# A mixture-of-experts and attention kernel: the memset between GpSimd's indirect DMAs, 128x256 in place of 128x512

## The chip, the cores and the metric

The kernel runs on one core of a Trainium2 chip. The metric is the device time of one execution in microseconds (us). In the profile the engines are called PE (TensorE), DVE (VectorE), ACT (ScalarE), POOL (GpSimd) and SP (SyncE); SP only issues DMAs. A name such as "SPq" is an engine's instruction queue, "PEld" is the loading of PE's weights.

## The reference

There are eight batch rows x of 1024 tokens and 256 features. Three steps are added to x in turn: half of a sparse feed-forward layer (FFN), an attention layer, and half of the same sparse FFN again, each on a layer-normalized input.

```python
x = x + 0.5 * ffn(layernorm(x))
x = x + attn(layernorm(x))          # windows of 64, plus 256 routed tokens a row
x = x + 0.5 * ffn(layernorm(x))

def ffn(x):                          # 8 experts of width 128, the best 2 of each token
    w = softmax(x @ router_w + router_b)
    mask = top_2_of(w) / sum(top_2_of(w))
    h = gelu(einsum('btd,nde->btne', x, W1) + b1)
    return sum_over_experts((einsum('btne,nef->btnf', h, W2) + b2) * mask)
```

## The kernel before, in words

The first FFN is computed sparsely, and this is where the change lies. The eight rows are dealt with in three batches, `BATCH = ((0, 2), (2, 5), (5, 8))`. For each row ACT and DVE normalize the tokens into `xb`, PE computes the router's logits, and DVE works out for every token the two places (`spot`) at which it shall stand in a list sorted by expert (`row_spots`, last line L1513). POOL then scatters the row to HBM: `send(r, i)` writes 128 tokens of `xb` to `spots_d` with one indirect DMA (L1952), 16 of them for a row (8 tiles of tokens, 2 experts each). Behind each send stands `pause`, which zeroes the scratch tile `apart`; nothing reads that tile.

When all sends of a batch have landed (`sent`, L613), SP loads blocks of 256 tokens, all of one expert, into `xin` (L617). The batches give 23, 31 and 31 blocks, 85 in all. For each block PE transposes (L863), multiplies by W1 (L872) and by W2 (L890), ACT computes the gelu (L1197), DVE adds the bias into `yout` (L1578), and SP stores it to `made_d` (L623). The loads run three blocks ahead through four buffers. `fetch(b, i)` on POOL gathers the results of row b back with an indirect DMA (L1976); the 16 fetches of row 0 are followed by `pause` too, those of later rows are not.

All engines go through one list of "ticks". Block s has tick 24 + s; row r starts at tick `ROW_AT[r]`, with `ROW_AT = (0, 6, 12, 18, 26, 33, 41, 49)`, its positions come 9 ticks and its sends 11 ticks later. So rows 0 to 2 are prepared before the first block and rows 3 to 7 between blocks. On SP the block load of tick t + 3 stands ahead of the row load of the same tick t. POOL has no other work than the sends between 35 and 251 us, and takes them in order of the rows.

After the blocks, from about 351 us, the attention layer runs (PE is the fullest engine), with scatters (`hs_d`, L1992) and fetches without `pause`, and then the second FFN, which is computed densely.

Of the kernel before, what the change touches and what calls it, by code (L numbers as in the profile page):

```python
# [8 lines left out]
F32 = mybir.dt.float32  # L9
# [9 lines left out]
P = 128  # L19
# [19 lines left out]
def build(nc, x_in, gamma_h, wq_h, wkv_h, wo_h, ln_g, ln_b, wqkv, wo_l, rt_q, rt_kv,  # L39
          router_w, router_b, w1, b1, w2, b2, out):  # L40
    pe, act, dve, pool, sp = nc.tensor, nc.scalar, nc.vector, nc.gpsimd, nc.sync
    ROWS, N, D = x_in.shape
# [27 lines left out]
    with ctx:  # L70
# [7 lines left out]
        def room(nbytes):  # L78
            at_ = top[0]
            top[0] += -(-nbytes // 32) * 32  # L80
            assert top[0] <= nc.sbuf_usable_end, (name_of_last[0], top[0], nc.sbuf_usable_end)
            return at_
# [3 lines left out]
        def at(name, shape, dt, offset):  # L86
            return nc.alloc_sbuf_tensor_at(name, shape, dt, offset=offset)
# [87 lines left out]
        xf_off = room(2 * C * 2 * P * 4)  # L175
# [55 lines left out]
        assert top[0] <= xf_off, (top[0], xf_off)  # L231


        apart = at("apart", [P, 2 * D], F32, xf_off)
        xb = [at(f"xb{i}", [P, T, D], F32, off) for i, off in enumerate((xt_off, xt_off + T * D * 4, y_off, yr_off + T * (D + 1) * 4))]
        zeros = at("zeros", [P, BT, D], F32, xt_off + 4 * TG * D * 4)
        assert 4 * TG * D + BT * D <= 2 * C * PADDED
# [1905 lines left out]
```

How the kernel before makes its waits and increments, by code:

```python
        def sent(engine, n):  # L575
            for r in range(*BATCH[n]):
                engine.wait_ge(s_sc[r % 4], 32 * T * (r // 4 + 1))
# [1 line left out]
        def made(engine, n):  # L580
            end = FIRST[n] + BLOCKS[n]
            for i in range(4):
                engine.wait_ge(s_bst[i], 16 * ((end - 1 - i) // 4 + 1))
# [10 lines left out]
            def row_load(r):  # L595
                if r >= 4:
                    sp.wait_ge(s_sc[r % 4], 32 * T * (r // 4))
                sp.dma_start(xb[r % 4][:, :, :], x_v[r]).then_inc(s_xa[r % 4], 16)
# [1 line left out]
            def pads(n, i):  # L600
                if n == 0 and i == 0:
                    sp.wait_ge(s_const, CONST)
                sp.wait_ge(s_tab, NTAB * (n + 1))
                for e in range(E // 2 * i, E // 2 * (i + 1)):
                    row = value(sp, pad_row[n][0:1, e:e + 1], 0, SPARE[n] - BLK)
                    sp.dma_start(spots_d[n][bass.ds(row, BLK), :].rearrange("(p s) d -> p s d", s=BT), zeros[:, :, :]).then_inc(s_zero, 16)
# [1 line left out]
            def block_load(s_):  # L609
                n = batch_of(s_)
                if s_ == FIRST[n]:
                    sent(sp, n)
                    sp.wait_ge(s_zero, 16 * E * (n + 1))
                if s_ >= 4:
                    sp.wait_ge(s_bT, s_ - 3)
                row = value(sp, block_row[n][0:1, s_ - FIRST[n]:s_ - FIRST[n] + 1], 0, SPARE[n] - BLK)
                sp.dma_start(xin[s_ % 4][:, :, :], spots_d[n][bass.ds(row, BLK), :].rearrange("(p s) d -> p s d", s=BT)).then_inc(s_bld[s_ % 4], 16)
```

## Time and profile before

| what | value |
|---|---|
| time, median of 3 runs | 2064.11 us (2062.43 to 2066.58) |
| the profiled execution | 2061.01 us, span 2059.2 us |
| busy over the span | PE 1875.1, DVE 1388.5, ACT 1203.6, POOL 1172.0 us |
| memsets of `apart` | 144, 78.0 us in all |
| indirect DMAs of `send` | 128, first start 35.32 us, last start 250.21 us |
| blocks | 85, first transpose 95.33 us, last at 346.3 us |

The span runs from the first instruction to the last. Busy time is the sum of an engine's instructions, without waits. An engine's idle time is shown in brackets before an instruction, with an arrow to what released it.

### The profile page before, as it was taken

To read this page: it belongs to the slowest core of one execution; us is meant where nothing else is said; L and a number is where in the kernel's file an instruction comes from. 1 tells how busy PE (TensorE), PEld (TensorE's weight loads), DVE (VectorE), ACT (ScalarE), POOL (GpSimd) and SP (SyncE) were. 2 spreads that over 40 slices of the span, in tenths; PEclk is the share of its full clock that TensorE was granted. 3 is DMA by queue.
4 is the path that set the end of the run, shared out by engine and by line. 5 is a ranking of instruction groups with operands and counts; after the bars stand their busy time and mean duration, and the time that the engine had idled before them with its cause. 6 is when DMAs were issued, how large, how long until landed. Compare 5 with 4: busy or idle time off the path is not lost.

```text
span 2059.2 us, 38092 instructions
## 1 busy us (share of the span) xinstructions
PE 1875.1 (91%) x11764; PEld 1398.7 (68%) x11764; DVE 1388.5 (67%) x4771; ACT 1203.6 (58%) x2974; POOL 1172.0 (57%) x1356
## 2 busy tenths in 40 slices
PE   3488899889989989989989989989999999999998
PEld 1166678656656666666666666666666788888887
DVE  5355457756855865875874875775754488888887
ACT  5487567565565565565566566566555555555554
POOL 3999852662772782782682683583453444444444
PEclk8599999999999999999999999999999999999999
DMA  6688887200310310310310220220121111111110
GB/s 200 248 267 289 275 267 251 67 27 1 100 40 1 98 42 1 95 45 1 93 47 1 81 55 5 77 57 8 37 63 82 38 42 42 42 42 42 36 38 21
DMA packets 103841, 168.15 MB, mean 82 GB/s; under 512 B 13249, under 2 KB 64857, under 8 KB 102745
## 3 DMA queue, kind: packets, MB, share of 16 engines
q1 hardware_dynamic: 80600, 112.91, 16.8%
q0 software_dynamic: 20736, 52.52, 8.1%
q8 instruction: 97, 1.59, 0.3%
q14 instruction: 104, 0.84, 0.1%
q10 hardware_dynamic: 2304, 0.28, 0.1%
HBM read 80.33 MB, written 85.34 MB: 80 GB/s over the span
## 4 chain that ended last, share of the span: by engine, by line
PE 51%; DVE 16%; POOL 10%; issue 10%; ACT 9%; DMA 4%; ACTq 0%; SPq 0%; DVEq 0%; POOLq 0%
PE bank L730 7%; PE bank L732 6%; PE bank L731 6%; PE bank L1022 4%; PE bank L1011 4%; PE bank L982 4%; PE bank L993 4%; PE bank L953 3%; PE bank L890 2%; ACT prob L1319 2%; PE bank L872 2%; POOL prob L2005 2%; DVE st L1412 2%; POOL spots_d L1952 2%; PE bank L984 2%
## 5 line engine op out<-in xcount | busy, mean ns | idle before, releaser
L2005 POOL TENSOR_TENSOR prob<-prob,rden 128x512 f32<-128x512 f32 x320 | 337.6, 1056 | 453.8 <-DVE rden L1798 450.2
L1319 ACT ACTIVATE prob<-prob,nmax 128x256 f32<-128x256 f32 x512 | 256.0, 502 | 391.3 <-DVE nmax L1780 383.5
L1780 DVE CUSTOM_DVE_ANT_0 prob<-bank,mask 128x256 f32<-128x256 f32 x512 | 195.3, 417 | 103.3 <-PE bank L982 97.3
L1666 DVE SCALAR_TENSOR_TENSOR xb<-bank,gate,xb 128x256 f32<-128x256 f32 x512 | 211.8, 476 | 55.6 <-PE bank L732 55.1
L1932 POOL TENSOR_TENSOR hl<-hf,hh 128x512 fp32r<-128x512 f32 x128 | 164.7, 1291 | 113.8 <-ACT hh L1122 109.1
L982 PE MATMUL bank<-kT,qT 64*128 64x256 f32 x1024 | 211.2, 431 | 14.3 <-DVE nmax L1780 13.6
L993 PE MATMUL bank<-ident,prob 128*128 128x128 f32 x1280 | 198.8, 278 | 16.1 <-POOL prob L2005 16.1
L993 PEld LDWEIGHTS bank<-ident,prob 128*128 128x128 f32 x1280 | 154.3, 142 | 73.7 <-POOL prob L2005 26.5
L1121 ACT ACTIVATE hf<-bank,b1s 128x512 f32<-128x512 f32 x128 | 88.2, 689 | 171.2 <-PE bank L732 167.7
L1792 DVE COPY probT<-bank 128x512 f32<-128x512 f32 x160 | 110.0, 688 | 113.7 <-PE bank L993 112.8
L1011 PE MATMUL bank<-probT,V 128*64 128x128 f32 x2048 | 169.7, 287 | 9.0 <-ACT oT_s L1335 7.1
L1992 POOL DMA_INDIRECT hs_d<-yr,place x128 | 130.0, 1016 | 43.4 <-issue 31.0
L1952 POOL DMA_INDIRECT spots_d<-xb,spot x128 | 126.3, 987 | 49.4 <-DVE spot L1513 28.4
L1011 PEld LDWEIGHTS bank<-probT,V 128*64 128x64 f32 x2048 | 108.2, 137 | 64.5 <-issue 61.3
L730 PE MATMUL bank<-w,hh 128*128 128x256 f32 x512 | 146.6, 286 | 3.7 <-POOL hl L1932 2.6
L982 PEld LDWEIGHTS bank<-kT,qT 64*128 64x128 f32 x1024 | 94.0, 186 | 77.7 <-issue 47.1
L732 PE MATMUL bank<-w,hh 128*128 128x256 f32 x512 | 144.7, 283 | 0.0
L731 PE MATMUL bank<-w,hl 128*128 128x256 f32 x512 | 144.5, 282 | 0.0
L1812 DVE TENSOR_TENSOR x<-bank,x 128x256 f32<-128x256 f32 x64 | 27.0, 422 | 147.0 <-PE bank L1022 147.0
L1578 DVE TENSOR_TENSOR yout<-bank,b_all 128x512 f32<-128x512 f32 x85 | 58.1, 690 | 100.5 <-PE bank L890 62.0
L1022 PE MATMUL bank<-wol,oT_s 128*128 128x256 f32 x512 | 125.8, 388 | 0.0
L730 PE MATMUL bank<-xt_hi,wqkv_hi 128*128 128x512 f32 x256 | 114.1, 446 | 0.0
(256 smaller groups left out, 5044.7 us busy)
## 6 DMA issues: line engine op xcount, KB each, us to landing
xin<-spots_d SPq DMA_DIRECT2D x85, 256.0 KB
made_d<-yout SPq DMA_DIRECT2D x85, 256.0 KB
x<-in_L_attn_x SPq DMA_DIRECT2D x8, 1024.0 KB
x_d<-x SPq DMA_DIRECT2D x8, 1024.0 KB, 4.5
xb<-x_d SPq DMA_DIRECT2D x16, 512.0 KB, 3.9
out<-xb SPq DMA_DIRECT2D x16, 512.0 KB, 3.0
xb<-in_L_attn_x SPq DMA_DIRECT2D x7, 1024.0 KB, 6.7
spots_d<-zeros SPq DMA_DIRECT2D x24, 256.0 KB
```

Of the source, the lines that this page charges most:

```text
L730: pe.matmul(o, w[0], x[0], start=start, stop=False)
L731: pe.matmul(o, w[1], x[0], start=False, stop=False)
L732: return pe.matmul(o, w[0], x[1], start=False, stop=stop)
L982: ins = pe.matmul(bank[g % NS][:, 0:KEYS], qT[hs, hp, t * P:(t + 1) * P], kT[hs, hp, t * P:t * P + KEYS], start=True, stop=True)
L993: ins = pe.transpose(bank[3 + j % 2][:, (2 * h + kk) * P:(2 * h + kk + 1) * P], prob[j % NP][:, h, kk * P:(kk + 1) * P], ident[:, :])
L1011: ins = pe.matmul(bank[5][h * DH:(h + 1) * DH, hp * P:(hp + 1) * P], V[:, t + kk, hs] if t < T else hv[:, kk, hs], probT[j % 2][:, 2 * h + ...
L1022: ins = pe.matmul(bank[tb][:, 0:D], oT_s[:, ch, :], w[:, ch, :], start=(ch == 0), stop=(ch == HC - 1))
L1319: act.activation(prob[j % NP][:, h, :], src, ACT.Exp, bias=nmax[:, j % 4, h:h + 1], scale=-1.0 if light else 1.0, accum_out=den[:, j % 4, ...
L1666: dve.scalar_tensor_tensor(out=x, in0=bank[ob][:, (t % 2) * D:(t % 2 + 1) * D], scalar=gate[:, k % 2, t, e:e + 1], in1=x, op0=ALU.mult, op ...
L1780: ins = dve.tensor_tensor_reduce(prob[j % NP][:, h, :], bank[g % NS][:, 0:KEYS], mask[:, which, :], -1.0, 3e38, ALU.add, ALU.min, nmax[:, ...
L1952: pool.indirect_dma_start(spots_d[batch_of_row(r)], bass.IndirectOffsetOnAxis(spot[:, r, c, t:t + 1], 0), xb[r % 4][:, t, :], None).then_i ...
L2005: pool.tensor_tensor(prob[j % NP][:, :, :], prob[j % NP][:, :, :], rden[:, j % 4, :].unsqueeze(2).broadcast_to([P, 2, KEYS]), ALU.mult).th ...
```

## The change

The scratch tile `apart` is declared with 256 elements a partition and not 512. The memset in `pause` writes the whole tile, so each of its 144 executions writes half as much. Nothing else changes: no semaphore, no order, no DMA.

```diff
-        apart = at("apart", [P, 2 * D], F32, xf_off)
+        apart = at("apart", [P, D], F32, xf_off)
```

with D = 256, and its only use:

```python
            def pause(n):
                if n > 0:
                    pool.wait_ge(s_apart, n)
                pool.memset(apart[:, :], 0.0).then_inc(s_apart)
```

## Rows read from the trace of the kernel before

**Rows 1.** The page: busy tenths of POOL in 40 slices of the span.

```profile
POOL 3999852662772782782682683583453444444444
```

**Rows 2.** Windows by stage: length, busy time of each engine, clock, DMA share, GB/s.

```profile
35.00:92.00 57.00, 21.33 (x92) 10.99 (x90) 29.49 (x100) 31.30 (x57) 51.34 (x65) 0.62 0.50 186
92.00:182.00 90.00, 77.43 (x403) 52.80 (x403) 44.50 (x144) 65.41 (x129) 81.06 (x109) 0.96 0.82 273
```

**Rows 3.** Waits of SP's queue, 0 to 370 us: total, times, longest.

```profile
SPq L613 <- DMA spots_d<-xb,spot: 29.1, 2, 22.9
```

**Rows 4.** Timeline of POOL: start, duration, instruction, idle time before it.

```profile
35.32 2.20 POOL L1952 DMA_INDIRECT spots_d<-xb,spot  x1 [28.40 <-DVE spot L1513]
...
250.21 0.96 POOL L1952 DMA_INDIRECT spots_d<-xb,spot  x1 [0.17 <-issue]
...
254.55 0.20 POOL L2058 MEMSET xt_hi<- 128x128 f32 x1 [2.84 <-DMA spots_d<-xb,spot]
```

**Rows 5.** The chain that ended last, 88 to 96 us: start, duration, what.

```profile
87.88 0.97 POOL spots_d L1952
...
91.95 0.02 SPq L613
...
92.46 2.82 DMA xin<-spots_d
...
95.33 1.11 PE bank L863 x4
```

**Rows 6.** POOL's groups by form: count, busy us, mean ns, idle before.

```profile
L1958 POOL MEMSET apart<- 128x512 f32 x144 | 78.0, 541 | 0.1
...
L2027 POOL MEMSET zeros<- 128x512 f32 x1 | 0.5, 514 | 0.0
...
L2078 POOL MEMSET kT<- 128x256 f32 x1 | 0.3, 308 | 0.0
```

**Rows 7.** Timeline of POOL where no memset stands between indirect DMAs.

```profile
364.39 0.96 POOL L1992 DMA_INDIRECT hs_d<-yr,place  x1 [0.30 <-ACT yr L1237]
365.66 1.05 POOL L1992 DMA_INDIRECT hs_d<-yr,place  x1 [0.30 <-ACT yr L1237]
```

**Rows 8.** Timeline of DVE: positions of rows 1, 3, 4 and 7.

```profile
51.77 0.46 DVE L1513 CAST spot<-spot_f 128x16 uint32<-128x16 f32 x1
...
111.42 0.17 DVE L1513 CAST spot<-spot_f 128x16 uint32<-128x16 f32 x1
...
139.37 0.17 DVE L1513 CAST spot<-spot_f 128x16 uint32<-128x16 f32 x1
...
221.07 0.45 DVE L1513 CAST spot<-spot_f 128x16 uint32<-128x16 f32 x1
```

**Rows 9.** Timeline of SP's queue: a store, and the load of block 23.

```profile
165.65 0.32 SPq L623 DMA_DIRECT2D made_d<-yout  x1
172.90 0.35 SPq L617 DMA_DIRECT2D xin<-spots_d  x1
```

**Rows 10.** Timeline of PE: two block transposes that waited for their load.

```profile
182.23 0.66 PE L863 MATMUL bank<-ident,xin 128*128 128x128 f32 x4 [0.75 <-DMA xin<-spots_d]
...
273.09 0.68 PE L863 MATMUL bank<-ident,xin 128*128 128x128 f32 x4 [2.40 <-DMA xin<-spots_d]
```

**Rows 11.** The chain that ended last, 263 to 279 us.

```profile
263.31 9.73 DMA xin<-spots_d
...
273.77 1.71 PE bank L890 x4
...
277.60 0.87 PE bank L890 x4
```

**Rows 12.** Windows around the start of batch 2.

```profile
240.00:255.00 15.00, 12.46 (x61) 10.64 (x60) 3.64 (x6) 6.79 (x15) 11.00 (x19) 0.89 1.00 341
255.00:275.00 20.00, 17.60 (x95) 15.15 (x94) 5.34 (x8) 11.08 (x25) 17.85 (x26) 0.96 0.95 321
...
273.00:277.00 4.00, 3.91 (x13) 3.09 (x14) 0.78 (x2) 0.60 (x1) 3.58 (x6) 0.57 1.02 390
```

## The prediction, on record before the result

> **What bounds the kernel now.** I read the slices of the page first, because the edit touches one GpSimd instruction and the question is where that engine sets the pace. POOL is nearly full in slices 2 to 5 and half idle later [rows 1]. A table by stage follows: from 35 to 92 us POOL is busy 51.3 of 57 us while PE has 21.3; from 92 us on POOL is as full (81.1 of 90 us), but PE has 77.4 of the 90 and the blocks run, with the DMA engines busy 0.82 of the time [rows 2]. So there are two regimes, and a GpSimd saving is worth something different in each.
>
> The waits of the DMA queue on SP name the place of the first regime: SP waits at L613 (`sent`, in front of the first block load of a batch) for the scatters, twice, 29.1 us in all, 22.9 us the longer [rows 3]. The timeline of POOL shows what it waits for. The first send starts at 35.32, the 128th at 250.21 with a gap of 0.17 us before it [rows 4], and each is a DMA_INDIRECT with one `apart` memset behind it. (250.21 - 35.32) / 127 = 1.692 us per send. Batch 0 has two rows, 32 sends. The chain of waits says that this reaches the end: the last send of batch 0, its DMA, the first `xin` load (2.82 us), the first block transpose at 95.33 [rows 5], before which PE had nothing to do. From there on the ticks (the 85 blocks and the preparation of rows 3 to 7) stand in program order behind that first block, so what the start gains, all that follows gains, unless something else ends a wait.
>
> **The memset's price.** The changed tile has 256 elements a partition. `apart` at 512 takes 0.541 us on average; a halo of `kT` is a memset of 128x256 f32 at 0.308; `zeros`, 128x512, took 0.514 on a quiet chip [rows 6]. Saving: 0.541 - 0.308 = 0.233 us. Bounds: 0.514 - 0.308 = 0.206, if the 0.027 that `apart` takes above `zeros` stays; 0.541 / 2 = 0.27, if all of it scales. I take 0.233, the row with exactly the new shape. As a page has it: the Trainium skill (GPSIMD Engine Reference, Elementwise — side-by-side cycle accounting) puts a simple body at 1.03 cycles an element at 1.2 GHz; an estimate from it is 256 x 1.03 / 1.2 GHz = 0.220 us, by which the first term below would be 6.8 us; the trace's own two shapes give 0.206 to 0.233 and decide.
>
> **Does the period shrink by it?** Where no memset stands between, as at 364.39 and 365.66, indirect DMAs start 1.27 us apart, 0.96 us of work and a gap of 0.30 [rows 7]. That is the nearest floor. The new period would be 1.692 - 0.233 = 1.459 us, above 1.27, so nothing seen here stops it. All of the saving then shortens POOL's sequence.
>
> **Batch 0 (the main term).** Between the starts of the first and the last of 32 sends lie 31 memsets: 31 x 0.233 = 7.2 us (6.4 and 8.4 by the bounds). The inputs are there: POOL now comes to row 1 at 35.32 + 16 x 1.459 = 58.7, and row 1's positions stand at 52.2 [rows 8]. SP's wait of 22.9 us leaves 15.7 before anything else on its queue can come last. The first block starts at 88.1 in place of 95.3. The load of row 4 stands behind the first block load on SP, so it moves along too.
>
> **Batch 1.** Rows 3 and 4 have positions (L1513) only after PE has done blocks: 111.6 and 139.5 us, row 7's at 221.5 [rows 8]. Moved by 7.2 these are 104.4 and 132.3. POOL reaches row 3 at 35.3 + 48 x 1.459 = 105.4, so it doesn't wait; it is through row 3 at 128.7 and waits 3.6 us for row 4. Here POOL stops being the bound. The last send of batch 1 starts at 132.3 + 15 x 1.459 = 154.2 and has landed about 4 us later, as the last of batch 0 did (87.88 to 91.95), at 158.3. SP now finishes its store at 165.98 and can load block 23 only at 172.90 [rows 9]; moved by 7.2 it comes at 158.8. The 6.2 us wait of SP goes. For PE it was worth little, as loads run three blocks ahead: one wait of 0.75 us at 182.23 [rows 10]. Term: 0.75 us, between 0 and 0.75.
>
> **Batch 2.** Its sends have landed when the halo memset starts at 254.55 [rows 4], and the load of block 54 is issued at 263.31 [rows 11]: 8 us of slack already, so sends that end sooner give nothing by themselves. With the last row's positions at 221.5 - 8.0 = 213.5 its last send starts at 235.4 and the slack is 15 us. 16 fetches (L1976) come next on POOL. 14 run now from 255.6 to 278, over the load of block 54, which takes 9.73 us; PE waits 2.40 us for it [rows 10, 11] and then runs 0.57 of its clock from 273 to 277 us [rows 12], the lower of its two levels (1.2 of 2.4 GHz) for most of it: 1.71 us for a group of four against 0.87 once warm [rows 11], so two such groups cost 1.7 more. The stall is worth 2.4 + 1.7 = 4.1 us. After the change the fetches run from 240.4, 1.42 us apart, to 260.2, and the load of block 54 is issued at 255.3: they lie over 5 of its 9.7 us, not over all; the load of row 0's x for the attention, which `attn_load` issues at tick 74, 4 blocks before (1024 x 256 values of 4 bytes, 1 MB), stays beside it. Bounds 0 and 4.1; nearer to no change, as the large load stays: 1.0 us.
>
> **After 351 us** there is no `apart` left and POOL's work is the same; the stage moves as a whole. The last 16 pauses, in the fetches, lie under the blocks (PE idle there is for block 54 alone): nothing for them.
>
> **Sum:** 7.2 + 0.75 + 1.0 = 9.0 us. The profiled execution took 2061.0 us (span 2059.2 and 1.8 around it), so 2052.0 on its own scale; the median of the runs shown is 3.1 us above, at 2064.1, and so **2055.1**.
>
> **The rivals.**
> (a) The stall at block 54 goes entirely, through a load freed of fetches: 7.2 + 0.75 + 4.1 = 12.1 us, and 13.3 with the upper memset bound: 2050.8 to 2052. For it: the DMA engines are at 0.95 to 1.0 in this stretch [rows 12], so 10 fetches less beside it count. Against: the x load of 1 MB stays. 0.17.
> (b) A part is given back. Between 240 and 255 us the DMA engines are at 1.00 [rows 12]; sends 16% denser (1.692 / 1.459) leave the block loads less. One more stall like block 54's costs 4.1: 9.0 - 4.1 = 4.9 us, 2059.2. For it: PE does wait for `xin` at two places [rows 10]. Against: 4 us pauses between rows appear from row 4 on, and total bytes are equal. 0.16.
> (c) The edit doesn't do what it says: the period is held by something else, descriptor making for instance, and the gap grows as the memset shrinks. Within 1 us of 2064.1. Against it stand the 1.27 us pairs [rows 7]; for it, that a gap after an indirect DMA is 0.30 and after the memset 0.16, of which 0.14 x 31 = 4.3 us could come back; with that partial form the gain is 9.0 - 4.3 = 4.7. Whole form 0.07.
> (d) Slower: the denser sends of batches 1 and 2 make PE run out of loaded blocks repeatedly, between 97 and 235 us, each time dropping its clock as at block 54. To lose by more than 4.1 us it must give back 13.1: four stalls of 4.1, 2064.1 - 9.0 + 16.4 = 2071.5. For it: the DMA engines at 0.82 [rows 2]. Against: with sends 1.692 us apart the wait at 182.23 was 0.75 us and cost no clock. 0.04. The page that would make it so: the Trainium skill (DMA: Bandwidth & Descriptors, Queues, rings and completion order) says that each DMA engine takes turns between the queues that have work, packet by packet, so the scatters' queue takes its share from SP's. The trace agrees that they compete, 9.73 us for block 54's load against 2.82 for the first.
>
> **How the numbers follow.** My forecast, a gain of 7 to 11 us (2053 to 2057), has 0.56, and the rivals the rest. The range reaches from (a) with the upper bound, 2050.5, over (b) and the partial form of (c), to 2060.0; what it leaves out is (c) whole, (d) and the tails. 0.2% is 4.1 us, about what this kernel's measurement can tell from no change. Faster takes the forecast, (a) and most of (b), 0.86; same takes (c) and the weak end of (b), 0.10; slower (d), 0.04.
>
> **What would show it.** `apart` at about 0.31 us and POOL's period at 1.46 (else (c)). SP's first wait for the scatters about 15.7 us in place of 22.9, the first transpose near 88; the second such wait gone. POOL idle some 3 us before row 4's sends. The blocks ended 8 to 12 us earlier, and the whole stage after them as long as before. If the blocks' stage is longer than now, counted from its own first transpose, it is (b) or (d), and the place is where PE waits for `xin`. The prediction is wrong above all if that stage stretches, or if a gap takes the memset's place.

## The result, and the profile after

The changed kernel took 2076.19 us (median of 8 runs, 2070.67 to 2080.96) where the kernel before, run beside it, took 2062.5 us (2060.2 to 2066.58): a ratio of 1.0066, 95% interval 1.005 to 1.0083. It is 13.7 us slower; 2055.1 us was forecast. The profiled execution took 2080.96 us with a span of 2079.2.

The same kernel, run again in two later sets of runs, gave two answers, and this matters for all that follows: 2078.95 us against 2062.96 in one set (1.0076, 1.0056 to 1.0096) and 2055.56 against 2060.64 in the other (0.9978, 0.9964 to 0.9991). So the document first reads the profile of the run on record, which lost time, then tells how the two answers differ in their traces.

**The start went nearly as forecast.** The groups of POOL's instructions on `apart` after, with the shortest, median and longest duration in ns, and its timeline at the first and at the second send:

```profile
L1958 POOL MEMSET apart<- x144: 317/326/338, 37.2 to 312.5; 128x256 f32 x144
```

```profile
34.96 2.20 POOL L1952 DMA_INDIRECT spots_d<-xb,spot  x1 [28.03 <-DVE spot L1513]
37.21 0.32 POOL L1958 MEMSET apart<- 128x256 f32 x1
37.69 0.97 POOL L1952 DMA_INDIRECT spots_d<-xb,spot  x1 [0.16 <-issue]
```

The memset went from 0.541 us to 0.326, a saving of 0.215 (0.233 forecast), and the gap behind it stayed 0.16: sends usually start 1.46 us apart, the number forecast. SP's queue, 0 to 375 us, waits once for the scatters and 16.9 us, where [rows 3] had two waits and 22.9 us:

```profile
SPq L613 <- DMA spots_d<-xb,spot: 16.9, 1, 16.9
```

The PE rows that waited for a block's load, against [rows 5, 10]: the first block transpose starts at 89.30 in place of 95.33, and of the rest two waited, 1.92 and 3.66 us.

```profile
89.30 1.11 PE L863 MATMUL bank<-ident,xin 128*128 128x128 f32 x4 [15.74 <-DMA xin<-spots_d]
...
250.71 0.66 PE L863 MATMUL bank<-ident,xin 128*128 128x128 f32 x4 [1.92 <-DMA xin<-spots_d]
...
256.75 1.12 PE L863 MATMUL bank<-ident,xin 128*128 128x128 f32 x4 [3.66 <-DMA xin<-spots_d]
```

The kernel before had three such waits behind its first block, 5.7 us in all: the two of [rows 10] and one that the prediction overlooked:

```profile
242.81 1.09 PE L863 MATMUL bank<-ident,xin 128*128 128x128 f32 x4 [2.54 <-DMA xin<-spots_d]
```

So PE waited as long for loaded blocks before (5.7 us) as after (5.6 us).

**Then the block stage stretched.** From the first transpose of block 0 to that of block 84 it takes 272.8 us (89.30 to 362.13), where it took 251.0 before (95.33 to 346.33). The 6.0 us are gone by block 12; block 53 starts 20.0 us later than before, block 84 15.8 us later. Behind block 84 both kernels need about the same (1717 and 1713 us to the end of the span; the traces of all kernels here have 1708 to 1717). The windows of after, against the second line of [rows 2]:

```profile
92.00:182.00 90.00, 72.60 (x375) 51.55 (x374) 43.49 (x142) 61.49 (x120) 63.38 (x99) 0.94 0.76 253
182.00:273.00 91.00, 75.21 (x375) 56.55 (x373) 36.74 (x100) 50.03 (x102) 64.44 (x104) 0.92 0.72 244
```

PE has 72.60 busy us where it had 77.43, and no other engine took its place: DVE, ACT and POOL all have less (POOL also by its shorter memsets), and the DMA share fell from 0.82 to 0.76. No engine's load explains the loss; the engines wait longer. Who is waited for is in the view of waits, 85 to 300 us (total us, times, longest):

```profile
DVE yout L1578 <- remote: 53.1, 13, 6.0
DVE yout L1578 <- PE bank L890: 43.1, 22, 5.2
POOL spots_d L1952 <- DVE spot L1513: 33.3, 4, 9.6
...
ACT hf L1197 <- remote: 10.9, 7, 1.7
ACT xa L1163 <- remote: 10.2, 6, 4.1
```

"remote" is a releaser that the view can't name; in the same stretch of the kernel before there is no such row. In the four rows with DVE `yout` and ACT the wait is for a result of PE; POOL in the third row waits for positions, which DVE works out from PE's logits. One of these waits on the timelines of PE and of ACT shows what it is:

```profile
117.29 1.37 PE L826 MATMUL bank<-ident,xb 128*128 128x128 f32 x8 [1.38 <-issue]
118.49 0.60 PE L863 MATMUL bank<-ident,xin 128*128 128x128 f32 x4
```

```profile
118.78 0.60 ACT L1176 ACTIVATE xh<-bank 128x512 f32<-128x512 f32 x1 [0.22 <-remote]
121.74 1.32 ACT L1163 ACTIVATE xa<-bank 128x512 f32<-128x512 f32 x2 [2.37 <-remote]
```

PE's transposes for `xa` (L826) end at 117.29 + 1.37 = 118.66. ACT is idle for 2.37 us and copies them only at 121.74, 3.1 us after their end; the update that it waits for is recorded at 121.72. I set every recorded semaphore update that only PE gives against the end of the last PE group that gives it and had ended (my own reading of the trace's updates; "late" is over 0.1 us). Of those from about 90 to 280 us, where sends and fetches go, 66% are late in after: the median of all is 0.97 us, that of the late ones 2.0, the latest 5.82. Before, 2% are, at most 0.34. Counted up to block 84, which adds 80 us with three fetches and no send, the share in after is 41%. Updates of ACT, DVE and POOL stay within 0.06 us in both. In the block stage the late ones lie only where POOL issues sends or the fetches behind them: 2.8 us is the median from 105 to 131 us, and once the last send of the row is through (130.31 + 0.96 = 131.27) five come in a heap, at 132.08, 132.14, 132.20, 132.26 and 132.32.

### The profile page after: what moved, and what is told of

Same layout as the page of the kernel before. It is cut to its first block, busy times and chain, and to the rows that moved or that the text cites. A ratio compares the mean times of both kernels' runs of the same rounds, so it can differ in the third digit from the quotient of the medians.

```text
span 2079.2 us, 38092 instructions
## 1 busy us (share of the span) xinstructions
PE 1884.8 (91%) x11764; PEld 1402.2 (67%) x11764; DVE 1390.0 (67%) x4771; ACT 1206.1 (58%) x2974; POOL 1144.7 (55%) x1356
## 4 chain that ended last, share of the span: by engine, by line
PE 50%; DVE 17%; issue 10%; POOL 9%; ACT 9%; DMA 3%; another core or an unknown queue 2%; SPq 0%; DVEq 0%; ACTq 0%; POOLq 0%
PE bank L730 7%; PE bank L732 6%; PE bank L731 6%; PE bank L1022 4%; PE bank L1011 4%; PE bank L982 4%; PE bank L993 4%; PE bank L953 3%; ACT prob L1319 2%; PE bank L890 2%; PE bank L872 2%; POOL prob L2005 2%; DVE st L1412 2%; DVE x L1591 2%; POOL spots_d L1952 2%
## 5 line engine op out<-in xcount | busy, mean ns | idle before, releaser
L993 PE MATMUL bank<-ident,prob 128*128 128x128 f32 x1280 | 199.2, 279 | 16.9 <-POOL prob L2005 16.9
```

The lines of the kernel that those rows point to most:

```text
L993: ins = pe.transpose(bank[3 + j % 2][:, (2 * h + kk) * P:(2 * h + kk + 1) * P], prob[j % NP][:, h, kk * P:(kk + 1) * P], ident[:, :])
```

## The experiments

Runs of one set ran under one chip number, the kernel before beside them. The sets fall into two kinds:

- kind one: the runs on record, experiments 1 to 4, 5 to 8, and 17 and 18. Kernels with close sends have late updates.
- kind two: experiments 9 to 11, 12, and 13 to 16. No PE update was over 0.02 us late, whatever the kernel.

A mark that does not depend on the pause that is varied tells the kinds apart. Between 351 and 2040 us scatters of `hs_d` and fetches follow one another without `pause` in every kernel alike. There each of the 12 traces of kind one, that of the kernel before included, has 5 to 9 PE updates over 0.1 us late (the latest 1.73 us in the kernel before, 3.95 in experiment 7), and each of the 8 traces of kind two has none.

The kernel before hardly tells them apart by time (2062 to 2063 against 2059.7 to 2061.2 us). The expectations of experiments 9 to 12 were written before I knew this. In the table, "stage" is from the first transpose of block 0 to that of block 84, "spacing" the usual time between the starts of two sends, "late" and "latest" tell of PE's updates from about 90 to 280 us.

```
kernel                        kind  ratio   95% interval      us       spacing     block 0  stage   late   latest
before                        1     -       -                 2062.5   1.67        95.3     251.0    2%    0.34
256 (the change)              1     1.0066  1.005 to 1.0083   2076.19  1.46        89.3     272.8   66%    5.82
1  256 in batch 0 only        1     0.9968  0.9954 to 0.9982  2055.55  1.67 later  88.5     251.6    2%    0.39
2  two memsets of 256         1     1.002   1.0008 to 1.0031  2064.6   1.71        94.6     252.4    3%    0.59
3  384                        1     0.9987  0.9977 to 0.9998  2060.15  1.56        91.9     251.4    8%    0.73
4  none                       1     1.0392  1.0371 to 1.0412  2139.93  1.27        94.4     330.3   34%   13.0
5  256 in batches 1, 2 only   1     1.02    1.0181 to 1.0219  2103.15  1.46 later  94.2     294.6   60%   10.4
6  1024 after every 2nd       1     1.0016  1.0 to 1.0032     2064.54  1.27, 2.1   94.1     256.8   10%    1.36
7  320                        1     1.0049  1.0029 to 1.0068  2071.79  1.51        89.0     262.6   57%    4.13
8  128 in batch 0 only        1     0.9978  0.9966 to 0.999   2056.6   1.67 later  90.5     249.2    1%    0.40
9  512, more PE updates       2     0.9999  0.9983 to 1.0014  2060.32  1.67        94.1     251.7    0%    0.02
10 groups of 8                2     0.999   0.9976 to 1.0005  2057.26  1.27        91.8     248.3    0%    0.02
11 256, then 384              2     0.9968  0.9955 to 0.9981  2051.66  1.56 later  86.9     247.3    0%    0.02
12 groups of 16               2     0.9971  0.9955 to 0.9986  2056.67  1.27        89.2     250.2    0%    0.02
13 256 (the change)           2     0.9978  0.9964 to 0.9991  2055.56  1.46        88.7     253.0    0%    0.02
14 none                       2     0.9945  0.993 to 0.9959   2049.19  1.27        83.9     248.3    0%    0.02
15 groups of 16               2     0.9975  0.9963 to 0.9987  2054.97  1.27        88.9     246.9    0%    0.02
16 512, more PE updates       2     1.0002  0.9988 to 1.0015  2060.03  1.67        92.8     248.9    0%    0.02
17 256 (the change)           1     1.0076  1.0056 to 1.0096  2078.95  1.46        87.0     267.6   62%    4.60
18 groups of 16               1     1.0364  1.0343 to 1.0386  2137.4   1.27        88.7     330.7   34%   13.81
```

The last four columns are of one execution each, which is not always a typical one: it took 2065.36 us in 7 and 2067.05 in 17, the shortest of their runs. The first send itself starts between 33.3 and 35.3 us.

**1. The short pause where no block runs yet.** Only the sends of batch 0 get 256 elements.

```diff
-                pool.memset(apart[:, :], 0.0).then_inc(s_apart)
+                width = D if n < 2 * T * 2 else 2 * D
+                pool.memset(apart[:, 0:width], 0.0).then_inc(s_apart)
```

> Edit: the memset of the scratch tile writes 256 elements in the 32 sends of batch 0 alone, and 512 in all others. Theory L (late signals): in the blocks' stage PE's semaphore updates come up to 4.6 us after its matmuls while POOL issues sends 1.46 us apart, and this costs the 22 us lost there; batch 0 is sent before that stage, so its 31 shorter memsets keep the whole gain: 6 to 7 us faster than before, about 2056, and no late updates after 90 us. Theory C (the denser scatters starve SP's block loads of the DMA engines) expects the same here, since the later sends are as sparse as before. If the earlier start itself loses the time (a shifted order of ticks), the result is slower than before, about 2070.

2055.55 us, 6.5 below the kernel before beside it. Block 0 starts at 88.5, the stage keeps its 251.6 us, and the "remote" waits are absent. This is most of the forecast gain at the start (6.5 of 7.2 us) without the loss behind it.

**2. Half as wide, but two of them.** Is it the narrow memset as such?

```diff
-                    pool.wait_ge(s_apart, n)
-                pool.memset(apart[:, :], 0.0).then_inc(s_apart)
+                    pool.wait_ge(s_apart, 2 * n)
+                pool.memset(apart[:, 0:D], 0.0).then_inc(s_apart)
+                pool.memset(apart[:, D:2 * D], 0.0).then_inc(s_apart)
```

> Edit: each pause is two memsets of 128x256 on the two halves of the tile, 0.33 us each, so a send is about 1.8 us from the next, a little more than before. Theory L with the interval as its cause: no late updates, 31 x 0.1 = 3 us slower than before, 2064 to 2067. Theory L with the short memset as its cause, whatever the interval: updates late again, 2070 or more. Theory C: as the interval, no loss in the blocks' stage.

2064.6 us, 2.5 above the kernel before beside it (1.0008 to 1.0031), with sends 1.71 us apart. The stage is about as long as before (252.4 us for 251.0) and no "remote" wait appears: a memset of 128x256 does no harm by itself, the spacing does.

**3. A width between.** `apart` with 384 elements.

```diff
-        apart = at("apart", [P, 2 * D], F32, xf_off)
+        apart = at("apart", [P, 384], F32, xf_off)
```

> Edit: width 384, memset about 0.43 us, a send every 1.57 us. Theory L says that there is a point between 1.46 and 1.69 us at which the late updates begin: if it lies below 1.57 the blocks start 3.5 us earlier and all is kept, 2059; if it lies above, part of the 22 us comes: 2063 to 2072. Theory C expects a loss in proportion to the density, 2064 to 2070, with waits of PE for its block loads.

2060.15 us at 1.56 us, 1.9 below the kernel before beside it. A few updates are late (8%), none by more than 0.73 us, and the stage does not grow.

**4. No pause at all.** This leaves the scratch writes out; the result is computed as before.

```diff
             def pause(n):
+                return
```

> Edit: no pause at all; sends follow one another, 1.27 us apart by the pairs seen in the attention stage. Blocks start 31 x 0.42 = 13 us earlier. Theory L: the lag is longer still than at 1.46, or lasts as long as sends go on, and takes back more than 22 us: 2075 to 2100. Theory C: the same sign, and PE's waits for its block loads grow. A gain (2050) would say that it is the memset, not the spacing of the indirect DMAs, that holds up PE's updates.

2139.93 us, 77.9 above before. Sends are 1.27 us apart, updates up to 13 us late, and now also ahead of the blocks: block 0 starts at 94.4 although the 32nd send starts at 75.2. In the windows of this run the DMA engines are much less busy than before (0.55, last but one column; 18 has the same), which speaks against the transfers as the cause:

```profile
92.00:182.00 90.00, 58.28 (x267) 40.04 (x268) 30.14 (x101) 43.98 (x86) 43.89 (x47) 0.78 0.55 183
```

**5. The complement of 1.** 512 in batch 0, 256 behind it.

```diff
+                width = 2 * D if n < 2 * T * 2 else D
+                pool.memset(apart[:, 0:width], 0.0).then_inc(s_apart)
```

> Edit: 512 elements in the 32 sends of batch 0, 256 in all later pauses, the complement of the run that gave 6.5 us. Theory L: nothing is gained before the blocks, and the late updates come in the blocks' stage as in the changed kernel, so the whole loss stands alone: 18 to 24 us slower than before, 2080 to 2086. If the loss came from the early start (ticks in another phase), this would be as before, 2062.

2103.15 us, 41.0 above before. So the loss needs no short pause in batch 0, and with 1 it lies with the close sends among the blocks. Its size, though, is not 13.7 + 6.5 = 20.2 but twice that (18 to 24 us were expected); why is open. The changed kernel did not run in this set, so a difference between sets is not ruled out.

**6. The same mean, every second gap the shortest.** A pause of 1024 elements after each second send; `apart` is declared that wide (not shown below).

```diff
-                if n > 0:
-                    pool.wait_ge(s_apart, n)
+                if n % 2 == 0:
+                    return
+                if n > 1:
+                    pool.wait_ge(s_apart, n // 2)
                 pool.memset(apart[:, :], 0.0).then_inc(s_apart)
```

> Edit: a pause only behind each second send, with 1024 elements, about 1.0 us: two sends 1.27 us apart, then one after 2.1, the same 1.69 us on average. If PE's updates are held up by a backlog that a mean rate builds, as before: 2060 to 2066, updates late by some tenths of a us at most. If each close pair holds them up until the next pause, but the pause clears them, single updates late by up to 1.3 us and 2062 to 2072.

2064.54 us. Pairs 1.27 us apart make 10% of the updates late, by 1.36 us at most, and the time is within 0.2% (1.0 to 1.0032). A close pair is nearly harmless.

**7. Between 256 and 384.** Width 320, as in 3.

> Edit: width 320, a send every 1.51 us, between 1.46 (late updates, 2076) and 1.56 us (none that count, 2060). A threshold in the interval: either as at 1.56, with 0.9 us more gained, 2059, or partly late, 2062 to 2070. A smooth cost in the interval would give 2068, the middle.

2071.79 us at 1.51 us, 57% late, at most 4.13. With 3 and the change this brackets the edge in sets of kind one: at 1.56 us nothing is lost, at 1.51 9.6 us, at 1.46 13.7. The three ran in three different sets.

**8. Batch 0 shorter still.** As 1, with `P` (128) in place of `D`.

> Edit: 128 elements in the pauses of batch 0, 512 in all others. A send every 1.36 us in batch 0. If PE has few enough updates before the blocks (rows 0 to 3 alone), they are not late enough to count and the blocks start 31 x 0.33 = 10 us earlier than before: 2052. With no pause at all updates were up to 8 us late before the blocks too; if 1.36 us is already so, the preparation of rows 1 to 3 slips and the gain falls to below that of 256 elements, 2055 to 2062.

2056.6 us, no better than 1. The 32nd send starts at 79.7, but PE's updates ahead of the blocks come up to 11.1 us late, and block 0 starts at 90.5, not sooner.

**9. More updates of PE at the old spacing.** Three more in each block, on a semaphore that nobody waits for. The first is shown; the others stand behind the first matmul with W1 and the first with W2.

```diff
                         ins = pe.transpose(tp[:, c, j * P:(j + 1) * P], xin[s_ % 4][:, j, c * P:(c + 1) * P], ident[:, :])
+                        if j == 0 and c == C - 1:
+                            ins.then_inc(s_extra)
```

> The kernel before (pauses of 512 elements, sends 1.67 us apart), with three more semaphore updates of PE in each block, on a semaphore that nobody waits for (after the first half of the block transpose, the first hidden matmul and the first output matmul). PE makes 67 updates between 92 and 182 us now; with the extra ones it would make some 150. Theory A (while GpSimd issues indirect DMAs, PE's updates are passed on at a limited rate, and what exceeds it queues up): the updates come late in the block stage although the sends are 1.67 us apart, waits that end by an unknown releaser appear in front of ACT and DVE, and the time rises, to 2068 to 2090 us. Theory B (only the spacing of the sends counts; at 1.67 us every update is passed on at once): no update is late, 2059 to 2066 us.

2060.32 us, none late. By the kind of its set this says nothing of sets that have late updates.

**10. Eight close sends, then a rest.**

```diff
-                if n > 0:
-                    pool.wait_ge(s_apart, n)
-                pool.memset(apart[:, :], 0.0).then_inc(s_apart)
+                if n % 8 < 7:
+                    return
+                for k in range(6):
+                    m = 6 * (n // 8) + k
+                    if m > 0:
+                        pool.wait_ge(s_apart, m)
+                    pool.memset(apart[:, :], 0.0).then_inc(s_apart)
```

> Eight sends without a pause between them, 1.27 us apart, and then six memsets of 128x512 in a row, so that the mean stays near 1.70 us a send. Theory A (a backlog that grows while sends are close and drains when they stop): the updates of PE are late inside a group, by 1 to 3 us, and prompt in the pause of 3.5 us; each block loses a little now and then, 2066 to 2076 us. Rival (the mean over a whole row is what counts, and short groups don't matter): 2060 to 2066 us. Rival (any stretch of sends 1.27 us apart costs as it does with no pause at all, where the updates were late by up to 13 us): 2090 us and more.

2057.26 us, none late. I first took this for a proof that short groups are harmless. It is not: its set is of kind two.

**11. 256 in batch 0, 384 behind it.** As 1, with `384` in place of `2 * D`.

> Pauses of 256 elements in batch 0, before the blocks run, and of 384 in the batches behind it. If the two gains add up (256 in batch 0 alone gave -6.5 us, 384 everywhere -1.9, of which some 3 us belong to batch 0 anyway): 2054 to 2058 us, not to be told from 256 in batch 0 alone. If the earlier start brings the sends of 1.56 us closer to where PE's updates come late: 2058 to 2064 us.

2051.66 us, 8.1 below the kernel before beside it.

**12. Sixteen close sends, then a rest.** As 10, with `n % 16 < 15`, `range(12)` and `12 * (n // 16)`.

> As the groups of eight, but sixteen sends (one row) 1.27 us apart and then twelve memsets of 128x512: the same mean of 1.70 us, the same number of sends, a stretch twice as long. In the kernel with no pause and in the one with pauses of 128, PE's updates were still prompt at the ninth send of a stretch and late by the fifteenth; in the groups of eight none was late. Theory (something behind the sends takes up the excess of about nine of them and only then holds PE's updates up, and it empties in a pause): the updates are prompt in the first half of each row and late by 1 to 4 us in the second, and the time rises to 2064 to 2080 us. Rival (only the mean over some tens of us counts, 1.56 us and more being harmless): no update is late, 2055 to 2062 us.

2056.67 us, none late. In 4 a row of sixteen sends at this spacing, after 11 us of rest, had an update 1.47 us late in its tenth send; here no row had any. The rows of sends are alike, so the kernel alone can't explain both, and that led to the next four.

**13 to 16. The old kernels again, on one chip.** The changed kernel, no pauses, groups of 16, more updates.

> The changed kernel again (pauses of 256 elements everywhere), beside the three kernels below and on one chip with them. If the late updates are the kernel's: 2072 to 2080 us, two in three of PE's updates late in the block stage, as before. If they belong to the chip or to an execution and not to the kernel alone: the time that the sum of the prediction gave, 2051 to 2058 us, and no update late.

> No pauses, again. If the late updates are the kernel's: 2130 to 2145 us, with updates late by up to 13 us. If they belong to the chip or to an execution: within some us of the kernel before or faster, 2045 to 2065 us.

> Rows of sixteen sends 1.27 us apart and then twelve memsets, again. If grouped sends are harmless and the other two kernels are not: 2053 to 2060 us and no update late here, late updates in the other two. If the chip decides: late updates and 2064 to 2090 us here as soon as the other two have them, none as soon as they have none.

> Pauses of 512 and three more semaphore updates of PE in each block, again. If the number of updates does not matter at 1.67 us: 2059 to 2066 us, none late, whatever the other three show. If it matters where updates are held up at all: late updates and 2068 us or more, on a chip on which the first two kernels have them.

The changed kernel: 2055.56 us in place of 2076.19. No pauses: 2049.19 in place of 2139.93. The instructions are the same, and so are the spacings, 1.46 and 1.27 us. The windows of the changed kernel here, and of the one without pauses, against those above:

```profile
92.00:182.00 90.00, 80.73 (x426) 56.50 (x425) 47.50 (x155) 67.83 (x134) 72.44 (x112) 0.97 0.85 287
```

```profile
92.00:182.00 90.00, 79.34 (x442) 57.83 (x443) 51.74 (x166) 69.60 (x139) 51.57 (x54) 1.00 0.83 279
```

PE has 80.73 busy us in place of 72.60, and 79.34 in place of 58.28. There are no "remote" waits, and the first row of the view of waits of the changed kernel, 85 to 300 us, is the plain one:

```profile
DVE yout L1578 <- PE bank L890: 77.9, 39, 5.2
```

**17 and 18. The control, and groups beside it.** The changed kernel a third time, and groups of 16.

> The changed kernel a third time, as the control for the next one. If the chip is of the kind of the first runs: 2070 to 2081 us, over half of PE's updates late in the block stage. If it is of the kind of the last ones: 2051 to 2059 us, none late. Nothing between the two is expected, if the chip decides.

> Rows of sixteen sends 1.27 us apart and twelve memsets, a third time. If the control has late updates: a build-up over close sends makes them late here in the second half of each row, 2064 to 2090 us; if only the mean spacing (1.70 us) counts, none is late and the time is 2053 to 2060. If the control has none late: 2053 to 2060 us whatever the mechanism, and the question stays open.

The control has late updates (2078.95 us), and beside it the groups of 16 cost 74.4 us, 2137.4 against 2062.96, though twelve memsets still follow each row. The same kernel had gained 4.6 and 5.7 us in 12 and 15. ACT's timeline in 18; the row of sends starts at 91.00 and ends at 111.2:

```profile
95.92 0.57 ACT L1176 ACTIVATE xh<-bank 128x512 f32<-128x512 f32 x1
...
100.72 0.60 ACT L1176 ACTIVATE xh<-bank 128x512 f32<-128x512 f32 x1 [2.00 <-remote]
...
109.92 0.60 ACT L1176 ACTIVATE xh<-bank 128x512 f32<-128x512 f32 x1 [5.38 <-remote]
```

The lateness builds up: the update at 96.56, in the fifth send of the row, is prompt; the one at 98.55, in the sixth, is 1.41 us late, one at 109.90, in the fifteenth, 6.62; at 113.58 one arrives that is 10.80 us old, with six others within 0.4 us, and from 115.64 on, in the memsets, all are prompt. So a rest of 7 us (111.2 to 118.4) does clear the heap, but only after the row has done its harm, and the mean of 1.70 us saves nothing.

## Why the prediction was wrong

**What held.** The memset's price was 0.215 us, not 0.233; it lies within the 0.206 to 0.27 given. The estimate of 0.220 from the Trainium skill (GPSIMD Engine Reference, Elementwise — side-by-side cycle accounting) was closer than the halo's row. The gap behind the memset did not grow and the usual period fell by the memset's saving, so rival (c) is out. That the new period came out at 1.46 us, the very number forecast, is luck: the forecast took 0.233 from 1.692, a mean over all sends that holds some longer ones, where the usual period before was 1.67 and 0.215 came off. SP's first wait fell to 16.9 us (15.7 forecast), the second went, and block 0 came 6.0 us sooner, not 7.2: 31 pauses of 0.215 are 6.7, and the 32 sends took 48.46 us in place of 54.23, which is 5.8. The other 0.9 went into single sends that took longer (up to 1.63 us, where 0.97 is usual). The send at 87.88 of [rows 5] is the 31st and not the last; the last starts at 89.55 and has landed 2.4 us later, not 4.

**The step that failed** is "From there on the ticks (the 85 blocks and the preparation of rows 3 to 7) stand in program order behind that first block, so what the start gains, all that follows gains, unless something else ends a wait", and, on the period, "nothing seen here stops it. All of the saving then shortens POOL's sequence". I had asked what the shorter pause frees, and looked for what could collide with it among the DMA queues only. In sets of kind one something else does end the waits: PE's semaphore updates reach their waiters late while sends are closer than about 1.56 us (the edge lies between 1.51 and 1.56). The stage grew by 21.8 us; less the 6.0 gained ahead of it, block 84 is 15.8 us late. The whole profiled execution, the slowest of its eight, was 20 us above that of before; by the medians the loss is 13.7. That it comes with close sends among the blocks and not with those of batch 0 is shown by 1 and 5; that it is spacing and not width, by 2; that it grows as the spacing shrinks, by 3, 7, 4.

**Rival (d)** had the sign (2071.5 us, chance 0.04) and the wrong mechanism. It let PE run out of loaded blocks, four times. PE's waits for `xin` behind block 0 did not grow: 5.7 us before, 5.6 after, and only 2.5 in 4, the slowest kernel. The DMA share fell, 0.82 to 0.76, and to 0.55 in 4. With (d) stood the rule of the Trainium skill (DMA: Bandwidth & Descriptors, Queues, rings and completion order) that queues take turns on a DMA engine; the loss here does not come by it, as the engines had more idle time than before. The same numbers refute **rival (b)**, whose one more stall is not there.

**Batch 1** looks like a sign of this and not its cause: POOL waited 9.27 us for row 4's positions where 3.6 was forecast. They wait in turn for PE's work on that row, which came later. In 13, without late updates, that wait is 3.43 us:

```profile
134.60 0.97 POOL L1952 DMA_INDIRECT spots_d<-xb,spot  x1 [3.43 <-DVE spot L1513]
```

**Where the updates are prompt, the working came out in kind and short in size.** In 13 the median is 2055.56 us, but the kernel before was faster there too, so the gain is 5.1 us (1.9 to 7.4 by the interval), not 9.0; that 2055.56 lies so near the 2055.1 forecast is luck. From the first send to block 0 it takes 54.5 us, against 59.2 and 59.4 in 9 and 16, which have pauses of 512 there: 4.8 us for 7.2 forecast, and about all of the gain. No run shows the 0.75 and the 1.0 us of batches 1 and 2. PE waits for `xin` behind block 0 for 5.3 us in 13:

```profile
238.92 1.11 PE L863 MATMUL bank<-ident,xin 128*128 128x128 f32 x4 [3.29 <-DMA xin<-spots_d]
270.07 0.66 PE L863 MATMUL bank<-ident,xin 128*128 128x128 f32 x4 [1.96 <-DMA xin<-spots_d]
```

The first of them is not a price of the denser sends, as rival (b) would have it. The kernel before has it (2.54 us at 242.81), and so have 9 and 16, with 6.0 and 5.5 us in all; the first line is of 9, the second of 16:

```profile
242.33 0.66 PE L864 MATMUL bank<-ident,xin 128*128 128x128 f32 x4 [3.67 <-DMA xin<-spots_d]
240.22 1.11 PE L864 MATMUL bank<-ident,xin 128*128 128x128 f32 x4 [2.52 <-DMA xin<-spots_d]
```

**What stays open.** What makes a set of one kind or the other: the results carry the chip numbers 10, 4 and 8 for kind one and 5 and 8 for kind two (the runs on record carry none), so the number 8 stands on both sides, and the chip as the cause is not shown. Whether the recording takes part: every timed run carries a recorded span and clock, and the traces of kind one hold fewer records; no run here was made with nothing recorded. Why only PE's updates are held up. Why 5 lost 41 us. Whether more PE updates (9, 16) or groups of eight (10) do harm in sets of kind one; neither ran there. Whether 11 and 14 are best depends on the kind: the kernel without pauses gains 11.5 us in one (14) and loses 77.9 in the other (4). Of the versions that ran where updates come late, 1 has the lowest ratio (0.9968) and beats both kernels; it did not run in a set of kind two, and 11 did not run in one of kind one.

## What to carry to other kernels

A pause between indirect DMAs that looks like waste can be what keeps other engines' signals prompt: shorten it first where no other engine is in a tight exchange with PE (batch 0 here), and look at the waits with an unnamed releaser after. When the busy time of the engines and the DMA share fall together, look for late signals, not for a busy resource. Repeat a surprising result in another set of runs before building a theory over it, and look in the trace for a part that no variant touches: here the same two kernels differed by 21 and 91 us between sets, while the kernel before differed by 2, and only the late updates in its untouched attention stage told the sets apart.

## What the runs showed of the hardware

- In some sets of runs (kind one), TensorE's semaphore updates come late while GpSimd issues a row of indirect DMAs, and those of ACT, DVE and POOL do not (within 0.06 us). In the block stage the latest was 0.73 us, at no cost, with 1.56 us from start to start, 4.1 us at 1.51, 5.8 (10.4 in experiment 5) at 1.46 and 13.8 at 1.27. The heap is gone 1 to 3 us after the sends stop (1.1 in the changed kernel, 2.6 in 18), one update each 0.06 us (132.08 to 132.32).
- It builds up: at 1.27 us a pair makes an update at most 1.36 us late; in a row of sixteen the first late update is in the sixth send in 18 and in the tenth in 4.
- In other sets (kind two; the chip numbers don't separate them) the same kernels show no update over 0.02 us late, and 128 sends 1.27 us apart run 11.5 us faster than with pauses of 512.
- The traces differ as well. The table of DMA issues gives a median time to landing for `xin` in 13 and none in the trace of after, and the count of recorded landings is 7,196 in after and 10,998 in 13, for the same instructions. The first line is of after, the second of 13:

```profile
xin<-spots_d SPq DMA_DIRECT2D x85, 256.0 KB
```

```profile
xin<-spots_d SPq DMA_DIRECT2D x85, 256.0 KB, 4.0
```

All traces of kind one hold fewer, 6,783 to 8,123 (the kernel before has the most), those of kind two 10,966 to 11,010. Whether missing records and late updates have one cause, no run here tells.
